# Layer 4 of a four-layer attention kernel: units of one batch and two heads, and values as three passes of high and low parts

## The chip, the core and the metric

The kernel runs on one core of a Trainium2 chip. Time is device time in microseconds for one execution of the whole program. A core has TensorE (matmuls and transposes into PSUM banks), VectorE, ScalarE and GpSimd, which work beside each other and are ordered by semaphores alone; SyncE issues the DMAs that stream weights in.

## What is computed

Four layers, each an attention block and a feed-forward block, over x of shape 8 x 128 x 512 and a context of the same shape. Only the fourth attention is touched:

```python
hidden_states = concatenate([context, latents], axis=1)       # 256 keys per batch
q = (latents @ Wq).reshape(b, q_len, N_KV_HEADS, N_GROUPS, HEAD_DIM)   # 4 x 8 heads of 128
k = (hidden_states @ Wk).reshape(b, kv_len, N_KV_HEADS, HEAD_DIM)
v = (hidden_states @ Wv).reshape(b, kv_len, N_KV_HEADS, HEAD_DIM)
scores = einsum('bqhgd,bkhd->bhgqk', q, k) / sqrt(HEAD_DIM)
out = einsum('bhgqk,bkhd->bqhgd', softmax(scores), v)
x = x + tanh(g_xattn[3]) * (out.reshape(b, q_len, 32 * 128) @ Wo)
```

Eight query heads in a row share one head of keys and values (a group); there are four groups. Behind it stands the last feed-forward block, a product with a dequantised 512 x 512 matrix.

## The kernel before

Products that need float32 precision are made in two ways. A full float32 matmul (`mm` with float32 operands) takes two records in the trace. `mm3` takes three matmuls of the reduced type `F32R`: each operand is split into a high part (a rounding copy) and a low part (the rest), and high by low, low by high and high by high are summed in PSUM. Layer 4 makes queries, scores and output with `mm3`, and values with full float32 matmuls of 128 moving columns.

Weights come as chunks of 128x512 through a ring of eight (`RING`): SyncE loads `raw`, GpSimd makes `w_hi` and `w_lo` (lines 614, 618), and TensorE frees a chunk by `w_free`, counted in `owed` and told on one of the next matmuls.

Layer 4 (`n == 3` in the code, `ATT[3]`, named L3) is cut into 128 units: a head by two batches, four units to a head. `run_steps` runs steps 0 to 129. In step k every engine goes through its own fixed list:

- TensorE (`attention(n)`, `step`): `scores(k)` into bank `S[k % 2]`; `turn(k - 1)`, four transposes of the probabilities into the bank `turned` (T); half a query piece (two of four contraction tiles, six matmuls of 512 columns) for a later head, in steps 0 to 123; `output(k - 2)`, two tiles of six matmuls together; `values(k - 1)` into the bank `value` (V).
- ScalarE: `pT` out of T for unit k-1 (line 1304), two exponentials for unit k (line 1519), in odd steps `q_hi`, then `a_hi` out of V for unit k-1.
- VectorE: `top`, the row maxima of unit k (line 2024); in four steps at each change of group a split of two batches of keys, `keys_split` (lines 1903, 1905); `reciprocal` and `g_inv` of unit k-1 (2046, 2049); two additions to `x` for unit k-2 (1970); `a_lo` for unit k-1 (2069); in odd steps `q_lo` (1911). At the end come the statistics of finished tiles (`tail_stats`, line 1703), the scale of the last norm for tiles 0 to 3 (`norm_scale`) and its first rows.

The waits that matter: values wait for `pT` and for the `a_hi` and `a_lo` of the unit before, since V is one bank; output waits for `a_hi` and `a_lo` of its own unit and for the addition that freed its bank; scores wait for `split`, which counts the split pieces of keys and queries in VectorE's order.

## Time and profile before

| | us |
|---|---|
| median of 3 runs | 2762.68 (2758.40 to 2764.48) |
| the profiled execution | 2762.54 |
| its span in the profile | 2760.7 |
| TensorE busy (matmuls) | 2682.1, 97% |
| VectorE busy | 1776.6, 64% |
| ScalarE busy | 1122.1, 41% |
| GpSimd busy | 839.7, 30% |

Layer 4's units run from 2105.5 to about 2722 us of the span; the last feed-forward block ends it. A busy share says that an instruction was in flight, not that the engine was at its peak. Durations of matmuls overlap: how far apart they start is the pace.

### The profile page before, as it was taken

What the parts mean: (1) busy time and instruction counts of PE and PEld (TensorE: products, weight loads), DVE (VectorE), ACT (ScalarE), POOL (GpSimd) and SP (SyncE); (2) the same over time, 40 slices, a digit from 0 to 9 for tenths busy, and PEclk for the clock granted to TensorE, in tenths of its full rate; (3) what the DMA queues carried; (4) which work ended last, traced back from release to release, by engine and by line L of the source; (5) the groups of instructions that cost most, each with busy time, mean ns of one, the idle gap of its engine ahead of it and who ended that gap; (6) DMA issues with size and microseconds to landing.
All of it is one profiled execution on the core that took longest, in us unless ns stands there. A gap on an engine that the chain in (4) does not pass through costs nothing.

```text
span 2760.7 us, 45251 instructions
## 1 busy us (share of the span) xinstructions
PE 2682.1 (97%) x14736; PEld 2264.1 (82%) x14736; DVE 1776.6 (64%) x3493; ACT 1122.1 (41%) x3088; POOL 839.7 (30%) x715
## 2 busy tenths in 40 slices
PE   6998999999999999999999999999999999999998
PEld 5886888888888887777888888788878888888887
DVE  5766545546446447777999999845553666666667
ACT  3542433333333333135666666421123444444442
POOL 4003433334324424323223222245523222222200
PEclk9999999999999999999999999999999999999999
DMA  5002111101101101111111111012211101110000
GB/s 149 17 5 67 43 35 50 38 29 51 42 23 53 42 27 46 37 38 39 31 34 30 34 30 33 29 47 61 58 45 40 28 28 28 32 28 28 28 5 31
DMA packets 59789, 106.01 MB, mean 38 GB/s; under 512 B 7184, under 2 KB 11536, under 8 KB 59536
## 3 DMA queue, kind: packets, MB, share of 16 engines
q1 hardware_dynamic: 56448, 96.49, 12.5%
q10 hardware_dynamic: 3216, 7.81, 0.8%
q8 instruction: 83, 1.36, 0.2%
q14 instruction: 42, 0.34, 0.0%
HBM read 100.09 MB, written 2.10 MB: 37 GB/s over the span
## 4 chain that ended last, share of the span: by engine, by line
PE 91%; DVE 6%; ACT 1%; issue 1%; POOL 1%; DMA 0%; DVEq 0%; ACTq 0%; POOLq 0%
PE four L651 50%; PE outp L651 25%; PE value L651 9%; PE turned L1016 4%; PE turned L773 1%; DVE stats L1703 1%; DVE x L1970 1%; PE value L698 0%; PE turned L698 0%; DVE probs L1732 0%; DVE nt L1665 0%; DMA raw<-in_stream 0%; PE turned L651 0%; DVE xt_lo L1737 0%; DVE probs L1850 0%
## 5 line engine op out<-in xcount | busy, mean ns | idle before, releaser
L614 POOL TENSOR_TENSOR w_hi<-raw,zero 128x512 fp32r<-128x512 f32 x347 | 372.6, 1074 | 1742.7 <-PE four L651 569.0
L1970 DVE SCALAR_TENSOR_TENSOR x<-outp,g_inv,x 128x512 f32<-128x512 f32 x768 | 548.6, 747 | 329.5 <-PE outp L651 328.6
L618 POOL TENSOR_TENSOR w_lo<-raw,w_hi 128x512 fp32r<-128x512 f32 x352 | 455.6, 1294 | 31.3 <-ACT w_hi L1304 4.2
L651 PE MATMUL four<-xt_hi,w_lo 128*128 128x512 f32 x1024 | 428.0, 418 | 3.9 <-DVE xt_lo L1737 3.2
L651 PE MATMUL four<-xt_hi,w_hi 128*128 128x512 f32 x1024 | 403.1, 394 | 0.0
L651 PE MATMUL four<-xt_lo,w_hi 128*128 128x512 f32 x1024 | 401.7, 392 | 0.0
L651 PE MATMUL outp<-w_hi,a_lo 128*128 128x512 f32 x800 | 327.1, 409 | 19.6 <-DVE a_lo L2069 10.4
L651 PE MATMUL outp<-w_hi,a_hi 128*128 128x512 f32 x800 | 316.7, 396 | 0.0
L651 PE MATMUL outp<-w_lo,a_hi 128*128 128x512 f32 x800 | 316.3, 395 | 0.0
L1519 ACT ACTIVATE probs<-probs,top 128x128 f32<-128x128 f32 x512 | 199.6, 391 | 213.6 <-DVE top L2014 127.4
L1304 ACT ACTIVATE pT<-turned 128x512 f32<-128x512 f32 x320 | 193.1, 603 | 203.4 <-PE turned L1016 145.6
L1304 ACT ACTIVATE a_hi<-value 128x512 fp32r<-128x512 f32 (+1 forms) x256 | 125.5, 490 | 339.1 <-PE value L651 339.1
L651 PEld LDWEIGHTS four<-xt_hi,w_hi 128*128 128x128 f32 x1024 | 192.9, 188 | 44.2
L2069 DVE TENSOR_TENSOR a_lo<-value,a_hi 128x512 fp32r<-128x512 f32 (+1 forms) x256 | 142.6, 557 | 129.0 <-ACT a_hi L1304 128.1
L651 PEld LDWEIGHTS four<-xt_hi,w_lo 128*128 128x128 f32 x1024 | 193.7, 189 | 36.8 <-issue 3.6
L651 PEld LDWEIGHTS four<-xt_lo,w_hi 128*128 128x128 f32 x1024 | 194.2, 190 | 31.1
L651 PEld LDWEIGHTS outp<-w_hi,a_lo 128*128 128x128 f32 x800 | 150.1, 188 | 83.5 <-issue 27.3
L651 PEld LDWEIGHTS value<-pT,v 128*128 128x128 f32 x1536 | 202.0, 192 | 17.2
L651 PE MATMUL value<-pT,v 128*128 128x128 f32 x1536 | 203.1, 275 | 0.0
L651 PEld LDWEIGHTS outp<-w_hi,a_hi 128*128 128x128 f32 x800 | 150.8, 189 | 36.8
L651 PEld LDWEIGHTS outp<-w_lo,a_hi 128*128 128x128 f32 x800 | 150.8, 189 | 29.0
L651 PE MATMUL four<-w_hi,ct_lo 128*128 128x512 f32 x416 | 167.2, 402 | 0.0
(299 smaller groups left out, 4911.1 us busy)
## 6 DMA issues: line engine op xcount, KB each, us to landing
raw<-in_stream SPq DMA_DIRECT2D x352, 256.0 KB, 2.6
ctx_raw<-in_ctx_t ACTq DMA_DIRECT2D x4, 512.0 KB, 6.2
x<-in_x_in ACTq DMA_DIRECT2D x2, 1024.0 KB, 10.6
kz<-kT SPq DMA_DIRECT2D x32, 64.0 KB, 2.7
pb<-in_position_bias ACTq DMA_DIRECT2D x1, 2048.0 KB, 9.2
out<-x SPq DMA_DIRECT2D x8, 256.0 KB, 2.0
qw<-in_qweight ACTq DMA_DIRECT2D x1, 768.0 KB, 3.9
ln_w<-in_ln_weight ACTq DMA_DIRECT2D x1, 256.0 KB, 2.6
```

The costliest lines, as they stand in the source:

```text
L614: pool.tensor_tensor(w_hi[:, k, :], raw[:, k % RAW, :], zero[:, :].to_broadcast([P, D]), ALU.add)\
L618: pool.tensor_tensor(w_lo[:, k, :], raw[:, k % RAW, :], f32(w_hi[:, k, :]), ALU.subtract)\
L651: m = pe.matmul(out_, l, r, start=start, stop=stop, skip_group_check=True)
L773: m = pe.transpose(T[:, tokens(j)], buf["pr"][:, u % 3, cols], ident[:, :])
L1016: m = pe.transpose(T[:, tokens(j)], probs[:, k % 2, tokens(j)], ident[:, :])
L1304: return act.activation(dst, src, ACT.Copy)
L1519: e = act.activation(probs[:, k % 2, cols], src[:, cols], ACT.Exp, bias=top[:, k % 2, j:j + 1], scale=1.0, accum_out=sums[:, k % 2, j:j + 1])
L1703: dve.bn_stats(stats[:, b, :], x[:, b, :]).then_inc(ln_tiny, 1)
L1970: dve.scalar_tensor_tensor(out=x[:, b, :], in0=O[no_f(k) % 2][:, :], scalar=scale, in1=x[:, b, :], op0=ALU.mult, op1=ALU.add)\
L2069: dve.tensor_tensor(buf["a_lo"][:, 0:w], V[:, 0:w], f32(buf["a_hi"][:, 0:w]), ALU.subtract).then_inc(s["a_lo"], 1)
```

## The change

1. A unit of layer 4 is now one batch and two heads that share keys and values: eight units to a pair of heads, still 128 units. Scores of a unit are two heads by the same 256 keys; output adds two tiles, from two weight chunks, to the same tile of `x`.
2. Query pieces are made in an order of pairs, in four slots; three instead of two are made ahead of step 0. The weight ring carries q, q, o, o for a pair instead of q, o for a head.
3. The values of a unit become one product of 256 moving columns (two heads by 128 queries) for each of two key tiles, as `mm3`: six matmuls of the reduced type instead of four full float32 products of 128 columns.
4. For that the turned probabilities get a high part (ScalarE's copy, now written as `F32R`) and a low part (`turned_lo`, a new subtraction on VectorE), and the values are split too (`values_split`, 16 pairs of a cast and a subtraction on VectorE). Values wait for `split` instead of `pT`. The split of keys stands behind the gate and `turned_lo` now.
5. `v_hi` lies over the space of `kT`, `v_lo` over that of `v`; the bias of the last block lies in the first keys and is loaded at step 34 instead of ahead of step 0.
6. The scale of the last norm for tiles 0 to 3 is made in step 127 instead of 128.

The diff, cut to its core:

```diff
@@ class Attention
-        self.NU = heads * units
+        self.together = 2 if name == "L3" else 1
+        self.NU = heads // self.together * units
-        self.nb = B // units
+        self.nb = self.together * B // units
@@
+            for i in range(self.NU + 1):
+                order += [("pT", i - 1)] if i else []
+                order += self.keys_split(i) + self.values_split(i) + self.pieces(i)
@@ prologue
-            self.first += vx[:4] + [w[0], w[1]] + vx[4:6] + [w[2], w[3]] + vx[6:] + q
+            self.first += vx[:4] + [w[0], w[1]] + vx[4:6] + [w[2], w[3]] + vx[6:]
+            self.first += [("q", 0, 0), ("q", 1, 0), ("q", 0, 1)]
@@ parts, splits
-        return [("q", t // 2, t % 2 * 2, 2)]
+        return [("q", self.query_piece(i)[1], i % 2 * 2, 2)]
+    def query_piece(self, i):
+        group, odd = divmod(i // 2 + self.ahead, 2)
+        return 2 * (group // 2) + odd, group % 2
+    def slot(self, what):
+        _, h, t = what
+        return (2 * (h // 2 * 2 + t) + h % 2) % 4
-        group, pair = divmod(i + 1, 8 * self.U)
-        return [("k", group, pair)] if i + 1 < self.NU and group and pair < 4 else []
+        group, at_ = divmod(i + 1, 4 * self.U)
+        return [("k", group, at_ // 2)] if i + 1 < self.NU and group and at_ in (0, 2, 4, 6) else []
+    def values_split(self, i):
+        group, at_ = divmod(i, 4 * self.U)
+        return [("v", group, at_ // 2)] if i < self.NU and at_ in (0, 2, 4, 6) else []
@@
-       Attention("L2", HEADS, 2, 8), Attention("L3", HEADS, 4, 0)]
+       Attention("L2", HEADS, 2, 8), Attention("L3", HEADS, 8, 0)]
@@ TensorE, scores
-                        for j, b in enumerate(L.batches(k)):
-                            cols = tokens(b % (B // 2))
+                        cols = tokens(b % (B // 2))
+                        for j, hd in enumerate(heads):
+                            slot = L.slot(("q", hd, b // 4))
@@ TensorE, turn
+                        if n == 3:
+                            pe.wait_ge(s["split"], L.split[("pT", k - 1)])
@@ TensorE, values
-                    elif k == 0:
-                        pe.wait_ge(s["j_out"], max(L.evac[("Vc", 0, B - 1)], L.evac[("Vx", 0, B - 1)]))
+                    else:
+                        group, b = k // (4 * L.U), k % L.U
+                        pe.wait_ge(s["split"], max(L.split[("pT", k)], L.split[("v", group, b // 2)]))
+                        for kt in range(2):
+                            both = slice(kt * 2 * P, (kt + 1) * 2 * P)
+                            m = mm3(V[:, 0:2 * P], (v_hi(group, b)[:, tokens(kt)], v_lo(kt, b, group)),
+                                    (buf["pT_hi"][:, both], buf["pT_lo"][:, both]), kt == 0, kt == 1, last=kt == 1)
+                        m.then_inc(s["values"], 1)
+                        return
...
-                            else:
-                                v = buf["v"][:, kt, b, tokens(h // 8)]
@@ ScalarE
-                        if kt == 0:
-
-                            act.wait_ge(FS[3]["wn"], 4)
-                            act.dma_start(M3["bias"][:, :], q_bias).then_inc(phase_in["F3"], 16)
-                        copy(buf["pT"][:, 0, :], T[:, :]).then_inc(s["pT"], 1)
+                        copy(buf["pT_hi"][:, :] if n == 3 else buf["pT"][:, 0, :], T[:, :]).then_inc(s["pT"], 1)
+                    if n == 3 and k == 4 * L.U + 2:
+                        act.dma_start(M3["bias"], q_bias).then_inc(phase_in["F3"], 16)
@@ VectorE
+                def values_split(what):
+                    _, group, pair = what
+                    rows = slice(2 * pair, 2 * pair + 2)
+                    v = buf["v"][:, :, rows, tokens(group)]
+                    hi = buf["v_hi"][:, group, rows, :].rearrange("p b (k t) -> p k b t", k=2)
+                    lo = buf["v_lo"][:, :, rows, tokens(group)]
...
+                    dve.tensor_copy(hi, v).then_inc(s["split"], 1)
+                    dve.wait_ge(s["split"], L.split[what] - 1)
+                    dve.tensor_tensor(lo, v, f32(hi), ALU.subtract).then_inc(s["split"], 1)
+                def turned_lo(u):
+                    dve.wait_ge(s["pT"], u + 1)
+                    dve.tensor_tensor(buf["pT_lo"][:, :], T[:, :], f32(buf["pT_hi"][:, :]), ALU.subtract)\
+                        .then_inc(s["split"], 1)
@@ VectorE, additions to x
+                        back = B if n < 3 else 1 if j else 2 * B - 1
-                        if no_f(k) > B:
-                            dve.wait_ge(s["x_acc"], at(L, lambda i: no_f(i) - B, k, it))
+                        if no_f(k) > back:
+                            dve.wait_ge(s["x_acc"], at(L, lambda i: no_f(i) - back, k, it))
@@ VectorE, tail_stats
+                        if n == 3 and k == L.NU - 1:
+                            norm_scale(range(B // 2), ln_base(norm + 1) + 6)
                         if n == 3 and k == L.NU:
-                            norm_scale(range(B // 2), ln_base(norm + 1) + 6)
@@ VectorE, step
-                    if n == 3 and k < L.NU:
+                    if 1 <= k <= L.NU:
+                        scaled_gate(k - 1, it, small)
+                    if n == 3:
+                        if 1 <= k <= L.NU:
+                            turned_lo(k - 1)
                         for what in L.keys_split(k):
                             keys_split(what)
-                    if 1 <= k <= L.NU:
-                        scaled_gate(k - 1, it, small)
+                        for what in L.values_split(k):
+                            values_split(what)
```

## Rows read from the trace of the kernel before

**Rows 1.** Page, chain that ended last, by engine: share of the span.
```profile
PE 91%; DVE 6%; ACT 1%; issue 1%; POOL 1%; DMA 0%; DVEq 0%; ACTq 0%; POOLq 0%
```

**Rows 2.** Busy time by stretch: length, each engine's busy us, granted clock, DMA share, GB/s.
```profile
2300.00:2500.00 200.00, 200.00 (x1245) 177.90 (x1245) 129.22 (x278) 91.11 (x269) 48.65 (x42) 1.00 0.10 27
```

**Rows 3.** Timeline of TensorE, one step: start, us, engine, line, operation, form.
```profile
2299.14 1.05 PE L651 MATMUL value<-pT,v 128*128 128x128 f32 x8
2299.95 0.36 PE L651 MATMUL four<-k_hi,q_lo 128*128 128x256 f32 x1
2300.15 0.28 PE L651 MATMUL four<-k_lo,q_hi 128*128 128x256 f32 x1
...
2300.74 0.60 PE L1016 MATMUL turned<-ident,probs 128*128 128x128 f32 x4
2301.10 0.48 PE L651 MATMUL four<-xt_hi,w_lo 128*128 128x512 f32 x1
...
2302.57 0.40 PE L651 MATMUL outp<-w_hi,a_lo 128*128 128x512 f32 x1
...
2303.98 1.05 PE L651 MATMUL value<-pT,v 128*128 128x128 f32 x8
```

**Rows 4.** Timeline of TensorE: last query piece ahead of step 0, then step 0.
```profile
2102.79 0.39 PE L651 MATMUL four<-xt_hi,w_lo 128*128 128x512 f32 x1
...
2105.51 0.28 PE L651 MATMUL four<-k_hi,q_lo 128*128 128x256 f32 x1
...
2106.23 0.39 PE L651 MATMUL four<-xt_hi,w_lo 128*128 128x512 f32 x1
```

**Rows 5.** Instructions by line and form, 2104 to 2760: busy us, mean ns, idle before.
```profile
L1737 DVE TENSOR_TENSOR xt_lo<-turned,xt_hi 128x512 fp32r<-128x512 f32 x4 | 2.7, 682 | 0.1
L1903 DVE CAST k_hi<-kT 128x512 fp32r<-128x512 f32 x12 | 5.0, 418 | 0.0
L1905 DVE TENSOR_TENSOR k_lo<-kT,k_hi 128x512 fp32r<-128x512 f32 x12 | 8.3, 693 | 0.4
L1703 DVE BATCH_NORM_STATS2 stats<-x 128x6 f32<-128x512 f32 x8 | 5.1, 680 | 0.0
```

**Rows 6.** Timeline of VectorE over the same step and into the next.
```profile
2300.65 0.42 DVE L2069 TENSOR_TENSOR a_lo<-value,a_hi 128x256 fp32r<-128x256 f32 x1 [0.55 <-ACT a_hi L1304]
2300.99 0.68 DVE L2024 TENSOR_REDUCE top<-four 128x2 f32<-128x512 f32 x1
2301.59 0.15 DVE L2046 RECIPROCAL inv<-sums 128x2 f32<-128x2 f32 x1
2301.78 0.23 DVE L2049 TENSOR_SCALAR g_inv<-inv,gate 128x2 f32<-128x2 f32 x1
2303.53 1.41 DVE L1970 SCALAR_TENSOR_TENSOR x<-outp,g_inv,x 128x512 f32<-128x512 f32 x2 [1.52 <-PE outp L651]
...
2305.83 0.68 DVE L1911 SCALAR_TENSOR_TENSOR q_lo<-four,q_hi 128x512 fp32r<-128x512 f32 x1
```

**Rows 7.** Timeline of ScalarE in the same step.
```profile
2300.23 0.39 ACT L1304 ACTIVATE a_hi<-value 128x256 fp32r<-128x256 f32 x1 [1.74 <-PE value L651]
2301.38 0.60 ACT L1304 ACTIVATE pT<-turned 128x512 f32<-128x512 f32 x1 [0.76 <-PE turned L1016]
```

**Rows 8.** Timelines of the layer's end: TensorE (step 122, last output), then VectorE.
```profile
2691.45 0.36 PE L651 MATMUL four<-k_hi,q_lo 128*128 128x256 f32 x1
...
2720.90 0.47 PE L651 MATMUL outp<-w_hi,a_lo 128*128 128x512 f32 x1 [1.13 <-DVE a_lo L2069]
...
2720.23 0.42 DVE L2069 TENSOR_TENSOR a_lo<-value,a_hi 128x256 fp32r<-128x256 f32 x1 [0.40 <-ACT a_hi L1304]
...
2724.08 1.00 DVE L1732 TENSOR_SCALAR probs<-x,mv,rstd 128x512 f32<-128x512 f32 x2
...
2727.51 0.67 DVE L1737 TENSOR_TENSOR xt_lo<-turned,xt_hi 128x512 fp32r<-128x512 f32 x1
```

**Rows 9.** Timeline of TensorE, first matmuls of the last block.
```profile
2730.70 0.63 PE L651 MATMUL outp<-wT_lo,xt_hi 128*128 128x512 f32 x1
```

More of the change, by code:

```diff
@@ L79, in early_chunks, with batches @@
         return []
+    def batches(self, i):
+        return list(range(B))
 class Attention:
@@ L111, in __init__ @@
                 u = i - self.lag_o
-                for b in self.batches(u):
-                    self.tile[(u, b)] = len(self.tile) + 1
+                for j in range(self.nb):
+                    self.tile[(u, j)] = len(self.tile) + 1
                 if u % self.U == self.U - 1:
-                    self.order.append(("o", u // self.U))
+                    self.order += [("o", h) for h in self.unit_heads(u)]
             if name == "L2":
@@ L123, in __init__ @@
         if name == "L3":
-            order = [("k", 0, pair) for pair in range(4)] + [("q", 0, 0), ("q", 0, 1)]
-            for i in range(self.NU):
-                order += self.keys_split(i) + self.pieces(i)
+            order = [("k", 0, pair) for pair in range(4)] + self.first[-self.ahead:]
+            for i in range(self.NU + 1):
+                order += [("pT", i - 1)] if i else []
+                order += self.keys_split(i) + self.values_split(i) + self.pieces(i)
             done = 0
             for what in order:
-                done += 2 if what[0] == "k" else 1
+                done += 2 if what[0] in "kv" else 1
                 self.split[what] = done
@@ L351, in build @@
             M3["u"] = sb("u", [P, KT, D], I32, st)
-        M3["bias"] = sb("q_bi", [P, D])
-        sb("behind_bias", [P, (KT - 1) * D])
+        q_lo = sb("q_lo", [P, 4, HALF], F32R)
         with ExitStack() as st:
@@ L381, in attention_buffers @@
         def attention_buffers(stack, n):
-            queries = {"qT": sb(f"qT{n}", [P, 2, TOK], F32, stack)} if n < 3 else \
-                {"q_hi": sb("q_hi", [P, 2, HALF], F32R, stack), "q_lo": sb("q_lo", [P, 2, HALF], F32R, stack)}
+            if n == 3:
+                return {
+                    "q_hi": sb("q_hi", [P, 4, HALF], F32R, stack),
+                    "q_lo": q_lo,
+                    "pT_hi": sb("pT_hi", [P, D], F32R, stack),
+                    "pT_lo": sb("pT_lo", [P, D], F32R, stack),
+                    "a_hi": sb("a_hi3", [P, 2 * P], F32R, stack),
+                    "a_lo": sb("a_lo3", [P, 2 * P], F32R, stack),
+                }
             return {
-                **queries,
+                "qT": sb(f"qT{n}", [P, 2, TOK], F32, stack),
                 "pT": sb(f"pT{n}", [P, 1, D], F32, stack),
@@ L437, in build @@
             A3 = attention_buffers(st, 3)
+            with ExitStack() as over:
+                A3["v_hi"] = sb("v_hi", [P, 4, B, 2 * P], F32R, over)
             A3["kT"] = sb("kT3", [P, 4, B, 2 * P], F32, st)
+            with ExitStack() as over:
+                A3["v_lo"] = sb("v_lo", [P, 2, B, D], F32R, over)
             A3["v"] = sb("v3", [P, 2, B, D], F32, st)
@@ L441, in build @@
             A3["k_lo"] = k_lo
+            M3["bias"] = A3["kT"][:, 0, 0:2, :].rearrange("p b t -> p (b t)")
             M3["sc"] = sb("q_sc", [P, KT], F32, st)
@@ L976, in scores @@
                     if n == 3:
-                        pe.wait_ge(s["split"], max(L.split[("q", h, t // 2)], L.split[("k", h // 8, t)]))
+                        heads, m, b = L.unit_heads(k), k // (4 * L.U), t
+                        pe.wait_ge(s["split"], max([L.split[("k", m, b // 2)]]
+                                                   + [L.split[("q", hd, b // 4)] for hd in heads]))
                     else:
@@ L1056, in output @@
                             continue
[L1057 removed]
+                        no = L.tile[(k, j)]
+                        if n == 3:
+                            c = chunk(lambda i: ("o", L.unit_heads(i)[j]), k, it)
                         if no > 2:
[L1060 removed]
+                            pe.wait_ge(s["x_acc"], at(L, lambda i: L.tile[(i, j)] - 2, k, it))
                         a = buf["a_hi"][:, tokens(j)], buf["a_lo"][:, tokens(j)]
                         mm3(O[no % 2][:, :], a, ring(c), True, True, last=True).then_inc(s["outp"], 1)
[L1063 removed]
+                        if n == 3 and k % L.U == L.U - 1:
+                            owed[0] += 1
+                    if n < 3 and k % L.U == L.U - 1 and len(L.batches(k)) - 1 in tiles:
                         owed[0] += 1
@@ L1433, in leave_bank @@
                     if kind == "q" and n == 3:
-                        dst, scale = buf["q_hi"][:, part, :], q_scale_
+                        dst, scale = buf["q_hi"][:, L.slot(what), :], q_scale_
                     elif kind == "q":
@@ L1699, in tile_stats @@
                     L = ATT[n // 2]
-                    dve.wait_ge(AS[n // 2]["x_acc"], max(t for (u, tb), t in L.tile.items() if tb == b))
+                    dve.wait_ge(AS[n // 2]["x_acc"], max(t for (u, j), t in L.tile.items() if L.batches(u)[j] == b))
                 else:
```

37 lines of the change are left out of this document (26 added, 11 removed).

## The prediction

> **What bounds the kernel now.** I read four views in this order. The chain of work that ended last says who decides the end: TensorE for 91% of the span, VectorE for 6% [rows 1]. The view by stretches, taken over 200 us of layer 4, shows TensorE busy for 200.00 of 200.00 us, VectorE for 129, ScalarE for 91, GpSimd for 49, at a granted clock of 1.00, which is the level of 2.4 GHz [rows 2]. So in this layer every other engine waits for TensorE, and what shortens TensorE's stream shortens the kernel until another chain becomes longer. The timeline of one step then gives the prices. A step is what TensorE issues for one unit: scores of unit k, transposes of unit k-1, half a query piece, output of unit k-2, values of unit k-1. I number steps from 0; there are 128 units.
>
> TensorE's step, by starts [rows 3]: values 2299.14 to 2299.95 (0.81 us, eight records for four products), scores 2299.95 to 2300.74 (0.79), transposes to 2301.10 (0.36), query half to 2302.57 (1.47), output to 2303.98 (1.41). From values to values that is 4.84 us; the same pattern repeats at 4.83 up to step 123. Durations in the rows are longer than these distances, since matmuls overlap; I use distances between starts for TensorE, and for VectorE wherever operations follow closely.
>
> **The values (the main term).** Removed: four products of 128 moving columns in full float32, 0.81 us. Added: two key tiles times three passes with 256 moving columns of the reduced type. Nothing like it writes the value bank now, but scores is the same form: 128 rows, 128 stationary columns, 256 moving columns, three passes of high and low parts, six in a row. There the first matmul takes 0.20 us to the second (2299.95 to 2300.15), the other five take 0.59 us up to the transposes, 0.118 each [rows 3]. The first one is the one that comes behind a full float32 matmul. In step 0 scores come behind a query matmul of the reduced type, and there all six take 0.72 (2105.51 to 2106.23), with no long first one [rows 4]. In the new order values come behind output and ahead of scores, all of the reduced type, so I take 0.118 for all twelve: 12 x 0.1175 = 1.41 us instead of 0.81 + 0.79 = 1.60. Gain 0.19 us a step. Bounds: 0.16 at step 0's pace, 0.10 if scores' first matmul keeps its 0.20, and 0.21 if the pace is a little better than the row.
>
> The trace has 0.118 us for a matmul of 256 columns of this kind at a clock of 1.00 [rows 3]. The Trainium skill (TensorE: Matmul & The Clock Gate, Back-to-back issue gap) gives 262 cycles at 2.4 GHz for 256 columns, 109 ns, and would make the six values 0.05 us shorter again, an estimate of some 6 us over the layer; the same rule misses scores as measured, so the row decides.
>
> The other parts of TensorE's stream keep their size. Scores now take two heads for one batch instead of one head for two batches: six loads and six matmuls as before. Output takes two tiles from two ring chunks instead of two tiles from one. The transposes write to other columns, 0.36 us either way. Query work is the same 64 pieces, but three instead of two are made before step 0: that is one piece more there, 2.72 us by the last piece ahead of step 0 (2102.79 to 2105.51 [rows 4]), and one fewer inside, so queries stop after step 121 instead of after step 123.
>
> **The low part of the turned probabilities (added work and a new wait).** VectorE gets one subtraction of 128x512 from the turned bank per step, and TensorE's values wait for it. The same operation on the same bank exists: xt_lo from turned, 682 ns [rows 5]; close behind others it costs 0.60, as top does (2300.99 to 2301.59); q_lo has top's duration and is taken alike [rows 6]. Queued behind it on VectorE: the splits, the two additions to x, a_lo, q_lo, top of the next unit. Who waits: values, and through x_acc and a_lo the next output.
> Is it in time? Let scores of step k start at 0; the new step is 0.705 scores, 0.36 transposes, 1.47 query, 1.41 output, 0.705 values, 4.65. Turned starts at 0.70; pT starts 0.64 behind it and takes 0.60 [rows 3, 7], so 1.94. VectorE comes from a_lo of unit k-2: values started at -0.70, their new length to the eviction is 0.91 (five distances of 0.118, 0.28 for the last, and the 0.04 that stands between the end of the values and a_hi now [rows 3, 7]), a_hi to a_lo 0.42 [rows 6, 7], so a_lo at 0.62, then 0.34, q_lo 0.60 in every second step, top 0.60, reciprocal and g_inv 0.33 [rows 6]: 2.5 at the latest. The subtraction ends at 3.15 and, with the 0.25 that TensorE takes from a_lo's end (2720.23 + 0.42) to output's start 2720.90 [rows 8], values could start at 3.4. TensorE arrives at 3.95. Slack 0.5 us in a step with q_lo, 1.1 in the other. As a loop over values: 0.91 + 0.42 + 0.34 + 0.60 + 0.60 + 0.33 + 0.68 + 0.25 = 4.13 against 4.65. So it costs nothing; without that cover each tenth beyond 0.5 costs 0.1 in every second step.
>
> The two additions now go to the same x tile, so the second waits for the first. They take 1.41 for both, and the first ends before the second output tile does (output tiles are 0.70 apart); a wait of VectorE on itself shows as 0.04 (reciprocal end 2301.75 to g_inv 2301.78 [rows 6]). I take 0.1 on VectorE, hidden. VectorE's step is then 0.34 + 0.60 + 0.33 + 0.60 + 1.5 + half of 0.60, 3.7 of 4.65.
>
> **The splits.** Values are split in 16 pairs of a cast and a subtraction. The keys' pair is the row: 418 and 693 ns [rows 5], at most 1.11. At each of three changes of group, key and value pairs alternate over eight steps, so VectorE has 3.7 + 1.1 = 4.8 in these steps against 4.65: up to 0.15 x 8 = 1.2 us of lag, spread over waits which have 0.3 to 0.8 us of room (the subtraction ends at 3.15 or 2.6, the first output tile at 3.4). Key pairs fall into steps where no q_lo stands ahead of top: 2.6 + 1.1 = 3.7, plus 0.25, ahead of the 4.65 at which scores need them. I take 0; the upper bound is 1.2 x 3 = 4 us.
>
> Other edits: the bias load moves to ScalarE's queue at step 34, into the dead part of the keys; it is one issue, and ScalarE is busy 91 of 200 us [rows 2]. The weight ring gets q, q, o, o instead of q, o; four chunks come free together at step 9 of each pair, while four others are ready, and GpSimd is busy a quarter of the time [rows 2]. Both nothing.
>
> **The start.** Step 1 needs the first subtraction: transposes at T, pT at T + 0.64, 0.60, subtraction 0.68, 0.25: 2.2 behind the transposes, TensorE arrives after 0.36 + 1.47 = 1.8 (no output yet). Loss 0.3.
>
> **The last steps.** Steps 122 to 127 have no query half: TensorE needs 3.2 and the loop decides. With one row of statistics (0.60 close behind others, 680 alone [rows 5]) in place of q_lo the loop is 4.13, as above. Measured from the start of step 122 (before: 2691.45 [rows 8]): values(121) 3.4; values(126) 3.4 + 5 x 4.13 = 24.0; in step 127 the norm's scale (2.2 us: from a_lo 2720.23 less 0.34 and two statistics of 0.60 to rows at 2724.08 is 2.3 [rows 8]) comes in, and top goes: values(127) at 24.0 + 4.13 + 2.2 - 0.6 = 29.8. Then a_lo 1.33 later, last output start 31.7 (before 29.45 = 2720.90 - 2691.45). From a_lo, before: 0.34, two statistics, scale, two rows of norm, two additions, two statistics, to xt_lo at 2727.51, 36.06 from step 122 [rows 8]. After: a_lo at 31.1, 0.34, one statistic, two rows of norm 0.95, and the additions, of which the second has to wait for the last output tile (31.7 + 1.65, so it runs from about 33.8 to 34.6), one statistic, xt_lo at 35.2. So the last stage starts 0.9 earlier than the old tail would give, though the last output is later: the scale has left the path. What is late next there is xt_lo itself and then row 2 of the norm, as now.
>
> **Sum.** Steps 2 to 121: 120 x 0.19 = 22.8. Step 1: +0.19 - 0.3 = -0.1. Query piece ahead: -2.7. Tail: +0.9. Together 20.9 us off the profiled execution's own 2762.54 (span 2760.7 and 1.8 around it), which stands at the median of the runs, 2762.68: 2741.7, I say 2742.
>
> **Rivals.**
> 1. The switch stays (chance 0.06). If the 0.20 of scores' first matmul comes from something other than its neighbour's type, 120 x 0.10 = 12.0 - 1.9 = 10 us: 2752. For: inside the steady steps the trace shows scores behind one kind of neighbour alone. Against: step 0 [rows 4].
> 2. VectorE cannot follow in places (0.12). The splits lag as bounded and the tail takes 0.5 us more in each of six steps: 4 + 3 = 7 us, 2749. For: VectorE has little idle time in those steps. Against: the reckoning of the waits above.
> 3. The slower one (0.04): the subtraction becomes the loop. Place: VectorE between pT and values. With q_lo the loop is 4.13 + d; from d = 0.52 it costs, and the average of a step passes the old 4.83 when 4.13 + d is 5.01, d = 0.88: the subtraction would have to take 1.56 instead of 0.68 us. At d = 1.3: 5.43 and 4.83 in turn, 5.13, 120 x 0.30 = 36 us slower, 2798. Against: 682 ns for the same form from the same bank [rows 5].
> 4. The gain is larger (0.10). 0.21 a step, and the last stage's first matmuls run at full pace: they take 0.63 us each now, where output's take about 0.40, ten such rows [rows 9], so 10 x 0.23 = 2.3. 25.2 - 2.8 + 0.9 + 2.3 = 25.6, 2737. For: the idle stretch ahead of them shrinks. Against: it does not go.
> 5. The edit does not reach the hardware as it reads, and nothing moves (0.02): 2760, within 0.2%.
>
> My forecast has 0.66. **Range:** 2736 to 2752 takes in rivals 1, 2 and 4 and leaves out 3 and 5 and what I have not seen. About 0.2% (5.5 us) is what a measurement of this kernel can tell from no change. Faster 0.94, same 0.02, slower 0.04.
>
> **What would show it.** In the timeline: values as six matmuls 0.118 apart, scores' six taking 0.705, a step of 4.65, no idle TensorE before values. Turned_lo at 0.68 us, ending half a microsecond before values start. In the waits: none of TensorE for VectorE in steps 2 to 121; in the last six, values waiting for pT_lo and steps of about 4.1. Wrong: a scores group that still takes 0.79, TensorE waiting for k_lo, or a step other than 4.6 to 4.7.

## The result, and the profile after

The changed kernel takes 2747.0 us (median of five runs, 2744.1 to 2748.9), the one before 2761.9 us on the same chip (2758.4 to 2764.5): ratio 0.9946, 95% interval 0.9935 to 0.9957. It ran twice more beside later experiments: 0.9954 (0.9941 to 0.9967) and 0.9950 (0.9937 to 0.9964). So it is faster by 0.5%, 11 to 15 us by the medians of the three comparisons; that is little, but every interval ends below 1. The forecast was 2742 with a range of 2736 to 2752. A single execution far off all others (8267.8 us, in the experiment with the low part for 8 of 512 columns) is in no figure here.

| | before | after |
|---|---|---|
| median, us | 2761.9 | 2747.0 |
| span of the profiled execution, us | 2760.7 | 2747.1 |
| start of step 0 of layer 4 | 2105.51 | 2109.98 |
| step 0, step 1 | 2.09, 3.83 | 2.09, 5.08 |
| steps 2 to 121, 120 steps | 580.02 | 564.37 |
| start of step 122 to the end | 69.25 | 65.58 |

The first three lines behind the span are read from the timeline of TensorE, as starts of the scores of a step; the last is the rest of the span. Between the two profiles lie -13.6 us: +4.5 up to step 0, +1.2 in steps 0 and 1, -15.7 in steps 2 to 121, -3.7 from step 122 on. Two later profiles of the same changed kernel differ from this one in three of these lines (below): step 1, steps 2 to 121 and the end.

The chain that ended last, by engine, of the changed kernel (it answers to [rows 1]), shows a little less TensorE and a little more VectorE:

```profile
PE 89%; DVE 7%; ACT 1%; issue 1%; POOL 0%; ACTq 0%; DMA 0%; DVEq 0%; POOLq 0%
```

Busy time by stretch, in the columns of [rows 2]: TensorE is still busy all the time at a granted clock of 1.00; VectorE has risen from 129 to 171 us in 200.

```profile
2300.00:2500.00 200.00, 199.88 (x1198) 174.75 (x1197) 171.07 (x335) 93.19 (x275) 53.65 (x45) 1.00 0.10 30
```

One step of TensorE after the change (it answers to [rows 3]):

```profile
2300.61 0.28 PE L698 MATMUL value<-pT_hi,v_lo 128*128 128x256 f32 x1
2300.72 0.28 PE L698 MATMUL value<-pT_lo,v_hi 128*128 128x256 f32 x1
...
2301.32 0.28 PE L698 MATMUL four<-k_hi,q_lo 128*128 128x256 f32 x1
2301.43 0.28 PE L698 MATMUL four<-k_lo,q_hi 128*128 128x256 f32 x1
...
2302.02 0.60 PE L1069 MATMUL turned<-ident,probs 128*128 128x128 f32 x4
2302.38 0.48 PE L698 MATMUL four<-xt_hi,w_lo 128*128 128x512 f32 x1
...
2303.85 0.39 PE L698 MATMUL outp<-w_hi,a_lo 128*128 128x512 f32 x1
...
2305.26 0.28 PE L698 MATMUL value<-pT_hi,v_lo 128*128 128x256 f32 x1
```

Six values take 0.71 us (2300.61 to 2301.32), six scores 0.70, and the long first matmul of scores, 0.20 in [rows 3], is gone. From values to values it is 4.65; over a long run of undisturbed steps 4.655. Nothing stands in brackets: TensorE waits for nothing.

The same step on VectorE (it answers to [rows 6]), with the new subtraction in it:

```profile
2300.16 1.61 DVE L2054 SCALAR_TENSOR_TENSOR x<-outp,g_inv,x 128x512 f32<-128x512 f32 x2 [0.33 <-issue]
2301.93 0.42 DVE L2158 TENSOR_TENSOR a_lo<-value,a_hi 128x256 fp32r<-128x256 f32 x1 [0.16 <-ACT a_hi L1367]
2302.28 0.68 DVE L2109 TENSOR_REDUCE top<-four 128x2 f32<-128x512 f32 x1
...
2303.29 0.69 DVE L1995 TENSOR_TENSOR pT_lo<-turned,pT_hi 128x512 fp32r<-128x512 f32 x1
2304.82 1.60 DVE L2054 SCALAR_TENSOR_TENSOR x<-outp,g_inv,x 128x512 f32<-128x512 f32 x2 [0.83 <-PE outp L698]
```

The subtraction ends at 2303.98, 1.28 us ahead of the values at 2305.26; in a step with q_lo it would be some 0.6 later, and still in time.

What was not foreseen is seen in the groups of VectorE from 2110 to 2680 us, by form; the last number before the bar is the mean in ns:

```profile
L1995 DVE TENSOR_TENSOR pT_lo<-turned,pT_hi 128x512 fp32r<-128x512 f32 x121 | 83.0, 686 | 0.1
L2138 DVE TENSOR_SCALAR g_inv<-inv,gate 128x2 f32<-128x2 f32 x121 | 36.2, 299 | 4.3
L1990 DVE TENSOR_TENSOR v_lo<-v,v_hi 128x512 fp32r<-128x512 f32 x16 | 14.3, 896 | 0.5
L1967 DVE TENSOR_TENSOR k_lo<-kT,k_hi 128x512 fp32r<-128x512 f32 x12 | 10.5, 872 | 0.4
```

k_lo was 693 ns before the change [rows 5]; its mean is now 872, and v_lo, of the same form, has 896. pT_lo, which reads PSUM beside its SBUF operand, is at 686 as forecast. Three of the twelve k_lo and three of the sixteen v_lo are long where the group changes, and one more v_lo at the start of the layer. VectorE and GpSimd in steps 33 and 34, first VectorE:

```profile
2264.38 0.42 DVE L1965 CAST k_hi<-kT 128x512 fp32r<-128x512 f32 x1
2264.82 1.41 DVE L1967 TENSOR_TENSOR k_lo<-kT,k_hi 128x512 fp32r<-128x512 f32 x1
...
2270.28 1.24 DVE L1988 CAST v_hi<-v 128x512 fp32r<-128x512 f32 x1
2271.56 1.65 DVE L1990 TENSOR_TENSOR v_lo<-v,v_hi 128x512 fp32r<-128x512 f32 x1
```

and GpSimd, which splits the weight chunks:

```profile
2264.52 1.16 POOL L661 TENSOR_TENSOR w_hi<-raw,zero 128x512 fp32r<-128x512 f32 x1 [6.33 <-PE outp L698]
2265.76 1.61 POOL L665 TENSOR_TENSOR w_lo<-raw,w_hi 128x512 fp32r<-128x512 f32 x1
...
2270.20 1.04 POOL L661 TENSOR_TENSOR w_hi<-raw,zero 128x512 fp32r<-128x512 f32 x1 [0.45 <-DMA raw<-in_stream]
2271.32 1.35 POOL L665 TENSOR_TENSOR w_lo<-raw,w_hi 128x512 fp32r<-128x512 f32 x1
```

Read them in turn. w_hi (1.04 alone, 1.16 here) ends at 2265.68; k_lo is recorded from 2264.82 to 2266.23, which is about the wait for that end and then its own 0.69. w_lo (1.29 alone) is recorded from 2265.76, waits for k_lo to end and takes 1.61. The cast v_hi waits for w_hi, and v_lo for w_lo. In each of these four the record is 0.14 to 0.15 us shorter than the wait plus the instruction's own time, so the sum holds to that much. One whole instruction waits for the other, and the record of the waiting one begins while it waits. The steps that hold this are 4.78 (33), 5.00 (34), 6.41 (35), 4.85 (36) and 4.82 us (38) long; in step 35 the output waited 1.17 us for a_lo:

```profile
2275.16 0.48 PE L698 MATMUL outp<-w_hi,a_lo 128*128 128x512 f32 x1 [1.17 <-DVE a_lo L2158]
```

The same is found at steps 65 to 70 and 97 to 102, though step 67 is 5.34 where step 35 is 6.41. In all, steps 2 to 121 take 564.37 where 120 x 4.655 is 558.6: 5.8 us lost. The Trainium skill (SBUF — State Buffer, SBUF: two separate sides) has a rule for it: VectorE and GpSimd share a pair of SBUF ports under an exclusive lock, which whichever instruction starts first holds to its end; on VectorE's side it concerns an instruction in a mode with two ports, or one with two SBUF inputs beside a GpSimd instruction that reads SBUF. By that rule k_lo and v_lo, with two SBUF inputs, are subject to it, and pT_lo, which has one input in PSUM, is free of it; the trace agrees (1.41 to 1.65 us for the subtractions that waited, 0.69 alone, and 0.68 to 0.69 for every pT_lo, GpSimd at work or not). The casts were stretched too, up to 1.24; by the rule they would be in a mode with two ports, which no row shows directly.

### The profile page after: what moved, and what is told of

Its sections match the earlier page's. It is cut to its first block, busy times and chain, and to the rows that moved or that the text cites. A ratio compares the mean times of both kernels' runs of the same rounds, so it can differ in the third digit from the quotient of the medians.

```text
span 2747.1 us, 45163 instructions
## 1 busy us (share of the span) xinstructions
PE 2664.0 (97%) x14480; PEld 2238.0 (81%) x14480; DVE 1893.6 (69%) x3653; ACT 1123.7 (41%) x3088; POOL 844.6 (31%) x715
## 4 chain that ended last, share of the span: by engine, by line
PE 89%; DVE 7%; ACT 1%; issue 1%; POOL 0%; ACTq 0%; DMA 0%; DVEq 0%; POOLq 0%
PE four L698 50%; PE outp L698 24%; PE value L698 9%; PE turned L1069 4%; PE turned L820 1%; DVE x L2054 1%; DVE stats L1765 1%; PE value L745 0%; PE turned L745 0%; DVE probs L1794 0%; DVE nt L1727 0%; ACT a_hi L1367 0%; DVE a_lo L2158 0%; PE turned L698 0%; DVE pT_lo L1995 0%
## 5 line engine op out<-in xcount | busy, mean ns | idle before, releaser
L2054 DVE SCALAR_TENSOR_TENSOR x<-outp,g_inv,x 128x512 f32<-128x512 f32 x768 | 560.0, 748 | 251.1 <-PE outp L698 225.9
L698 PEld LDWEIGHTS outp<-w_hi,a_hi 128*128 128x128 f32 x800 | 150.3, 188 | 35.9
L698 PE MATMUL four<-w_hi,ct_hi 128*128 128x512 f32 x416 | 163.1, 392 | 0.0
L698 PE MATMUL four<-w_lo,ct_hi 128*128 128x512 f32 x416 | 162.8, 391 | 0.0
L1367 ACT ACTIVATE pT<-turned 128x512 f32<-128x512 f32 x192 | 115.9, 604 | 106.9 <-PE turned L820 57.9
```

The lines of the kernel that those rows point to most:

```text
L698: m = pe.matmul(out_, l, r, start=start, stop=stop, skip_group_check=True)
L1367: return act.activation(dst, src, ACT.Copy)
L2054: dve.scalar_tensor_tensor(out=x[:, b, :], in0=O[no_f(k) % 2][:, :], scalar=scale, in1=x[:, b, :], op0=ALU.mult, op1=ALU.add)\
```

## The experiments

Ten more runs followed the first comparison, two of them of the changed kernel itself. The theory (A) was: the loop is TensorE's at 4.655, and what the sum lacks is lost where VectorE's splits meet GpSimd's. Its rivals: (B) VectorE has too little room for eight pairs of splits in some eight steps, whoever else works; (C) the gain comes from the units and the columns rather than from the passes; (D) the subtraction is not hidden at all.

### GpSimd kept away from the splits

```diff
+            def holds(k):
+                return 31 <= k < 103 and (k + 1) % 32 < 8
...
-                            owed[0] += 1
+                            (held if holds(k + L.lag_o) else owed)[0] += 1
```

A chunk that comes free in steps 31 to 38, 63 to 70 or 95 to 102 is handed on only after them.

> The changed kernel, but TensorE holds back the release of weight chunks that fall into steps 31 to 38, 63 to 70 and 95 to 102 until the step behind them, so GpSimd has no chunk to split while VectorE splits keys and values; VectorE's work is the same, eight splits in a row. Theory A (a split with both operands in SBUF, or the cast ahead of it, waits for GpSimd): k_lo and v_lo stay at 0.69 us instead of up to 1.65, the steps 33 to 38 take 4.65 to 4.75 instead of 4.78 to 6.41, and layer 4 gets about 5 us shorter: 2742. Rival B (VectorE simply falls behind with 1.1 us more in eight steps in a row): these steps stay between 4.8 and 5.3, at most 1.1 us is won: 2746.

Measured: 2746.6 us, ratio 0.9949 (0.9932 to 0.9966), so the median came out at B's 2746 and not at A's 2742. The trace says otherwise: steps 31 to 39 are all 4.65 to 4.66, steps 2 to 121 take 559.8 instead of 564.4. The groups of VectorE from 2255 to 2289.5 us:

```profile
L1975 DVE TENSOR_TENSOR k_lo<-kT,k_hi 128x512 fp32r<-128x512 f32 x4 | 2.8, 693 | 0.1
L1998 DVE TENSOR_TENSOR v_lo<-v,v_hi 128x512 fp32r<-128x512 f32 x4 | 2.8, 693 | 0.1
```

GpSimd has nothing to do from 2234.9 to 2289.8 there. Eight pairs in eight steps cost nothing with GpSimd idle, so B falls and A stands. A new loss of 0.35 us came at step 40 (also 72 and 104), where GpSimd makes up for its rest. There a VectorE operation on two columns, 0.23 us long elsewhere, waited behind GpSimd and made pT_lo late:

```profile
2296.40 1.14 DVE L2146 TENSOR_SCALAR g_inv<-inv,gate 128x2 f32<-128x2 f32 x1
2297.45 0.68 DVE L2003 TENSOR_TENSOR pT_lo<-turned,pT_hi 128x512 fp32r<-128x512 f32 x1
```

```profile
2296.22 1.30 POOL L665 TENSOR_TENSOR w_lo<-raw,w_hi 128x512 fp32r<-128x512 f32 x1
```

The median, on another chip than the first comparison's, shows 0.4 us of the 4.6 us that the steps win in the trace. Its four runs lie between 2743.7 and 2749.0, and its profiled execution took 67.9 us from step 122 to the end where the changed kernel's took 65.6, since its clock fell there (more of that below). So the steps carry the verdict here, not the median; that the time follows is shown only by the last experiments.

### The new units with values in full float32

```diff
-                            m = mm3(V[:, 0:2 * P], (v_hi(group, b)[:, tokens(kt)], v_lo(kt, b, group)),
-                                    (buf["pT_hi"][:, both], buf["pT_lo"][:, both]), kt == 0, kt == 1, last=kt == 1)
+                            m = mm(V[:, 0:2 * P], buf["v"][:, kt, b, tokens(group)], buf["pT_hi"][:, both],
+                                   kt == 0, kt == 1)
```

with turned_lo and values_split left away; the units, the query order and the ring of the change stay.

> The new units, query order and ring, but values as two full float32 matmuls of 256 moving columns, with no low part and no split of values. Theory: the gain is in the passes, not in the units or the 256 columns. Values take 0.81 to 0.86 us, scores' first matmul takes 0.20 again, a step is 4.83 to 4.88; against the kernel before the start loses 2.7 and the tail gives back 1 to 4 us: 2760 to 2768. Rival: 256 moving columns alone make it shorter, values 0.7 us or less, step 4.7, some 2748.

Measured: 2757.1 us, ratio 0.9981 (0.9971 to 0.9991), 3 us below the forecast; the step is 4.81, also a little below it. TensorE's values and the first two scores:

```profile
2303.85 1.03 PE L697 MATMUL value<-pT_hi,v 128*128 128x256 f32 x4
2304.53 0.47 PE L697 MATMUL four<-k_hi,q_lo 128*128 128x256 f32 x1
2304.83 0.28 PE L697 MATMUL four<-k_lo,q_hi 128*128 128x256 f32 x1
```

Values take 0.68 and scores' first matmul 0.30: 1.58 for both against 1.60 before. So 0.02 of the step is due to units and columns and 0.155 to the passes: six passes take 0.03 more than these values, and the long first matmul of scores, 0.18 over the pace here, goes. The rival was right that values take less than 0.7 us, but the first matmul of scores took 0.10 back, so C falls for the steady step. What pays there is that no full float32 stands between matmuls of the reduced type any more.

For the whole time C keeps a share. This kernel is 4.3 us below the one before, about a third of what the change gains: 2.8 us in steps 2 to 121 (577.2) and 5.5 from step 122 on (63.7), where a step takes 3.48 against 3.66 before and 4.10 in the changed kernel, less what is lost ahead of step 0. So the low part costs the changed kernel some 4 us from step 122 on (67.9 in its profiles with the clock fallen at the end, as it fell here), and what the units and the moved scale of the norm give there is several times the forecast's net +0.9. Why the new units shorten a step there from 3.66 to 3.48 was not looked into.

### The low part for 8 of 512 columns

```diff
-                    dve.tensor_tensor(buf["pT_lo"][:, :], T[:, :], f32(buf["pT_hi"][:, :]), ALU.subtract)\
+                    w = slice(0, 8 if u else D)
+                    dve.tensor_tensor(buf["pT_lo"][:, w], T[:, w], f32(buf["pT_hi"][:, w]), ALU.subtract)\
```

> The changed kernel, but from unit 1 on the low part of the turned probabilities is made for 8 of 512 columns, so the rest of it is stale; 0.5 us less on VectorE per step. Theory: VectorE is no bound in the steady steps, which stay at 4.655; the last six steps fall from 4.10 to 3.55, step 1 is unchanged (unit 0 is made whole), the changes of group lose less: 2747 - 3 - 3 = 2741. Rival: VectorE or the wait of values holds the steady steps, which then fall to 4.6 or less: 2735.

Measured: 2735.2, 2737.6 and 2741.7 us (forecast 2741), ratio 0.9924 (0.9903 to 0.9945). The steady step stays 4.655: the full subtraction is hidden there, and D falls. Where VectorE is the loop it shows: steps 122 to 126 take 3.57 instead of 4.10, so 0.53 is what all but 8 columns of the subtraction cost uncovered. The changes of group lost nothing either (4.65 to 4.66 in steps 32 to 39), although GpSimd splits as in the changed kernel: all k_lo and v_lo take 0.69. VectorE's work comes at other moments now and meets GpSimd elsewhere; VectorE, then GpSimd:

```profile
2264.29 0.86 DVE L2139 TENSOR_SCALAR g_inv<-inv,gate 128x2 f32<-128x2 f32 x1
...
2265.59 0.69 DVE L1990 TENSOR_TENSOR v_lo<-v,v_hi 128x512 fp32r<-128x512 f32 x1
```

```profile
2263.83 1.29 POOL L665 TENSOR_TENSOR w_lo<-raw,w_hi 128x512 fp32r<-128x512 f32 x1
2265.59 1.59 POOL L661 TENSOR_TENSOR w_hi<-raw,zero 128x512 fp32r<-128x512 f32 x1 [0.46 <-DMA raw<-in_stream]
```

Here v_lo was first and kept its 0.69, and w_hi waited: 1.59 instead of 1.04.

### The subtraction twice

```diff
+                    dve.tensor_tensor(buf["pT_lo"][:, :], T[:, :], f32(buf["pT_hi"][:, :]), ALU.subtract)\
+                        .then_inc(s["split"], 1)
+                    dve.wait_ge(s["split"], L.split[("pT", u)] - 1)
                     dve.tensor_tensor(buf["pT_lo"][:, :], T[:, :], f32(buf["pT_hi"][:, :]), ALU.subtract)\
```

> The changed kernel with the subtraction made twice, one behind the other: about 0.72 us more on VectorE between pT and values. By the prediction's slack of 0.5 us, steps with q_lo take 4.85 and the others 4.65, average 4.75, 60 x 0.2 = 12 us; the last six steps 4.8 each, 4 us; the changes of group, where VectorE then has 5.6 us of work per step, up to 20 us: 2747 + 36 = 2783. If the slack is really larger, 4.655 in the steady steps and 2771; if smaller, both kinds of steps get longer.

Measured: 2791.1 us, ratio 1.0115 (1.0094 to 1.0137), 8 us above the forecast. Steps with and without q_lo take 4.82 and 4.65 in turn, with ten of 5.4 and three of 5.17 outside the changes of group. Values wait for the second subtraction:

```profile
2303.46 0.36 PE L698 MATMUL value<-pT_hi,v_lo 128*128 128x256 f32 x1 [0.28 <-DVE pT_lo L1998]
```

This puts a number on rival 3 of the prediction. The second subtraction adds 0.72 (from start to start); 4.13 + 0.72 is 4.85, measured 4.82 (so the slack of 0.5 was rightly reckoned), and the last steps went from 4.10 to 4.82. So the loop over VectorE is 4.10 in the changed kernel, and a step with q_lo has 0.55 us of cover. Steps 2 to 121 take 600.3, 35.9 more, of which 60 x 0.17 = 10 us are the steps with q_lo; some 20 are at the changes of group, as forecast, where steps 31 to 39 are 5.2 to 6.3 us long; the steps of 5.4 were not foreseen.

### The changed kernel again, and the first values ahead of step 0

> The changed kernel once more, beside the three below, so that they are compared on the same chip. Nothing is altered. Expected: ratio to the kernel before 0.9946 again, within 0.001; step 1 about 5.1 us, steady steps 4.655, steps 33 to 38, 65 to 70 and 97 to 102 together 5.6 us over the even pace. The last block: its matmuls of 512 columns at 0.40 or at 0.63 us, by the granted clock of that execution; if the clock differs from that of the first profile, the 2.7 us that the end gained over the forecast are the execution's and not the change's.

Measured: 2749.1 us, ratio 0.9954 (0.9941 to 0.9967). With nothing altered, step 1 is 4.09 us and not 5.08. The changes of group lose 6.9 us and not 5.8, since step 67 is 6.44 here and was 5.34; the other long steps are the same to 0.02. In the first profile of the changed kernel, VectorE and GpSimd, and what TensorE made of it:

```profile
2112.89 1.56 DVE L1990 TENSOR_TENSOR v_lo<-v,v_hi 128x512 fp32r<-128x512 f32 x1
```

```profile
2112.86 1.04 POOL L661 TENSOR_TENSOR w_hi<-raw,zero 128x512 fp32r<-128x512 f32 x1 [0.29 <-DMA raw<-in_stream]
```

```profile
2116.36 0.36 PE L698 MATMUL value<-pT_hi,v_lo 128*128 128x256 f32 x1 [1.11 <-DVE pT_lo L1995]
```

In the second:

```profile
2113.16 0.69 DVE L1990 TENSOR_TENSOR v_lo<-v,v_hi 128x512 fp32r<-128x512 f32 x1
```

```profile
2113.29 1.46 POOL L661 TENSOR_TENSOR w_hi<-raw,zero 128x512 fp32r<-128x512 f32 x1 [0.45 <-DMA raw<-in_stream]
```

The chunk landed a little later, v_lo was first by 0.13 us, and the wait changed sides: GpSimd's cost nobody anything. Both of GpSimd's bracketed waits are for the chunk's DMA. So 1 us of step 1 hangs on the moment at which a transfer lands. My reading of 5.08 as a property of the kernel was wrong.

```diff
-            order = [("k", 0, pair) for pair in range(4)] + self.first[-self.ahead:]
+            order = [("k", 0, pair) for pair in range(4)] + [("v", 0, 0)] + self.first[-self.ahead:]
...
-        return [("v", group, at_ // 2)] if i < self.NU and at_ in (0, 2, 4, 6) else []
+        return [("v", group, at_ // 2)] if 0 < i < self.NU and at_ in (0, 2, 4, 6) else []
```

> The split of the first pair of values (a cast and a subtraction on VectorE, 0.42 and 0.69 us where nothing hinders them) is taken out of step 0, where GpSimd splits weight chunks, and put ahead of it, before the low part of the first query piece. Theory A (the two engines shut each other out): step 0 loses the cast of 0.84 and the subtraction of 1.56, the maximum of step 1 comes earlier by about their excess, and step 1 goes from 5.08 to 3.9 to 4.1 us; step 0 may start up to 1.1 us later, if the two operations are not covered by the query piece. Sum -1.0 (0 to -1.2) on a time of 2747. Theory B (step 1 is long because of the order of VectorE's work in it, whatever GpSimd does): step 1 keeps at least 4.6 us. The group changes are untouched and lose 5.6 us as before.

Measured: 2747.0 us, ratio 0.9948 (0.9935 to 0.9961); step 1 is 4.09 us. By itself that tells nothing, since the changed kernel reaches 4.09 as well. The moved pair still met GpSimd (the cast took 1.04 and the subtraction 1.66 us), but ahead of step 0, where the query pieces cover it. One profile can't show that step 1 is never 5.1 to 5.2 any more.

### Both remedies together, and VectorE's side moved instead

First the edit of the chunks and that of the first values in one kernel:

> Both remedies for the same cause: the first pair of values split ahead of step 0, and the chunks that are freed in steps 31 to 38, 63 to 70 and 95 to 102 handed to GpSimd only after the splits of keys and values in them. Expected if both losses come from GpSimd's splits beside VectorE's: step 1 4.0 us, steps 31 to 39 all 4.65, 0.35 us lost at each of steps 40, 72 and 104 (seen with the second remedy alone), so steps 0 to 122 take 1.0 + 4.6 = 5.6 us less than in the changed kernel, and the median is 2741 to 2742, ratio to the kernel before 0.9925. If the median shows less than 3 us against the changed kernel on the same chip, what the steps win is given back elsewhere (the end, or the granted clock), and the trace must show where.

Measured: 2745.7 us, ratio 0.9941 (0.9928 to 0.9954), 4 us above the forecast time, and 3.4 us below the changed kernel on the same chip; by the steps 5.4 (steps 2 to 121 take 560.1 against 565.5). It loses 0.5, 0.3 and 0.45 us at steps 40, 72 and 104 and 0.15 at 74. The 1 us of step 1 could not be won, since that profile of the changed kernel had 4.09 there already.

Then the chunks are left as the change has them, and the splits move (the first values stay ahead of step 0):

```diff
-        group, at_ = divmod(i + 1, 4 * self.U)
-        return [("k", group, at_ // 2)] if i + 1 < self.NU and group and at_ in (0, 2, 4, 6) else []
+        group, at_ = divmod(i + 4, 4 * self.U)
+        pair = {0: 0, 2: 1, 4: 2, 9: 3}.get(at_)
+        return [("k", group, pair)] if i + 4 < self.NU and group and pair is not None else []
```

and likewise `values_split`, with `i + 3` and `{0: 0, 2: 1, 7: 2, 9: 3}`.

> The other side of the same collision is moved: not GpSimd's splits of weights (the chunks are freed as in the changed kernel) but VectorE's splits of keys and values, out of steps 33 to 35 of each group's change: four of the eight to steps 28 to 31, the other ones to 32 and to 36 to 38; and the first pair of values is split ahead of step 0. Theory A (a lock between the two engines while both work from SBUF): the subtractions take 0.69 us at all or nearly all places, the changes of group lose at most 0.35 us in a few steps where a small operation of VectorE (g_inv, two columns) meets GpSimd's, and the median is 2741 to 2743. Rival (VectorE cannot take eight splits more in some ten steps, whatever GpSimd does): the steps that hold a split stay at 4.8 to 5.0 and 2 us or more are lost at each change.

Measured: 2742.5 us, ratio 0.9938 (0.9924 to 0.9952). Steps 33 to 39 are even; only steps 32, 64 and 96 are long, 5.13, which is 0.48 over the pace where at most 0.35 was expected. There the pair of step 31 still met a chunk; VectorE, then GpSimd:

```profile
2251.12 1.41 DVE L1994 TENSOR_TENSOR v_lo<-v,v_hi 128x512 fp32r<-128x512 f32 x1
```

```profile
2250.74 1.25 POOL L665 TENSOR_TENSOR w_hi<-raw,zero 128x512 fp32r<-128x512 f32 x1 [20.30 <-PE outp L702]
```

The last version puts the pairs into steps in which that trace shows GpSimd idle (`i + 5` with `{0: 0, 2: 1, 5: 2, 10: 3}` for keys, `i + 4` with `{0: 0, 2: 1, 8: 2, 10: 3}` for values):

> As the run before it (splits of keys and values out of steps 33 to 35, first pair of values ahead of step 0), but with the second pair of values out of step 31 too, where its subtraction took 1.41 us behind GpSimd's split of a chunk and step 32 became 5.13 us. Pairs now in steps 27, 28, 29, 30, 32 and 36 to 38 of each change of group; by the trace of the run before GpSimd is idle from 2230.4 to 2250.7 (steps 27 to 30) and from 2253.7 to 2260.4 (step 32). Theory (a whole-instruction lock between VectorE's splits and GpSimd's): all v_lo and k_lo of the changes 0.69 us, step 32, 64 and 96 at 4.65, steps 2 to 121 within 0.5 us of 120 times 4.655, 558.6, median 1 to 1.5 us lower than that kernel's, 2741. If the subtraction is long in other steps instead, the theory or my reading of where GpSimd works is wrong.

> The changed kernel a third time, as the comparison on the same chip. Nothing is altered: ratio to the kernel before 0.9950 within 0.001; steps 33 to 38 and the like lose 5.6 us again. Step 1 either 4.1 or 5.1 us, by whether GpSimd's next chunk has landed before VectorE's subtraction starts; the stretch from step 122 to the end either 65.6 us (granted clock 1.00 in it) or about 67.9 us (clock fallen).

Measured: 2741.8 us, ratio 0.9933 (0.9920 to 0.9946), against 2747.1 us, ratio 0.9950 (0.9937 to 0.9964), for the changed kernel on the same chip. Steps 2 to 121 take 558.9 against 565.5, and not one of them is off the pace. Its groups of VectorE from 2110 to 2680 us:

```profile
L1994 DVE TENSOR_TENSOR v_lo<-v,v_hi 128x512 fp32r<-128x512 f32 x15 | 10.4, 693 | 0.5
L1971 DVE TENSOR_TENSOR k_lo<-kT,k_hi 128x512 fp32r<-128x512 f32 x12 | 8.3, 693 | 0.4
```

It does the same work as the changed kernel, with the same matmuls, and only the steps of the splits differ. So the splits' loss is GpSimd's doing and is won back whole in the steps. In time, this version's interval lies wholly below 1, so it beats the kernel before; against the changed kernel it is 5.3 us better in the median, but the intervals of the two ratios overlap, and there the trace carries the verdict. Against the version ahead of it, which ran on another chip, its ratio is 0.0005 lower, which the intervals can't tell from none. In the third profile of the changed kernel the splits lost 6.9 us again, step 1 was 5.20 us, and from step 122 to the end it took 67.9.

## Why the prediction was right, and which terms were off

**The values.** Right. Six matmuls 0.118 apart, scores' first one at the same pace, nothing idle. The gain is 4.833 - 4.655 = 0.178 a step and not 0.19: I had taken single distances of one step (4.84) where the mean of 120 is 4.833. 120 x 0.178 is 21.4 for 22.8.

**Rival 1 (the switch stays)** did not happen: the first matmul of scores is 0.118 ahead of the second in the steady steps. The 262 cycles for 256 columns of the Trainium skill (TensorE: Matmul & The Clock Gate, Back-to-back issue gap), which the page gives for a single matmul without its weight load and which would have made the values 0.05 us shorter, are not seen either: the row decided rightly.

**The low part.** Right: 686 ns, no wait of TensorE for it in the undisturbed steps. The loop reckoned from rows was 4.13; the last steps, where nothing covers it, measure 4.10, and the kernel without most of the subtraction 3.57. The two additions to the same tile take 1.60 and not 1.5, hidden.

**The splits.** This is the term that failed. I took 0 with 4 as the upper bound, and it is 5.8 us in the first profile and 6.9 in the two others. The bound came from VectorE's capacity alone (4.8 us of work in a step of 4.65); the run with GpSimd held back shows that this part costs nothing. I took the pair's 1.11 us from rows in which GpSimd happened not to interfere [rows 5] and dismissed the ring's new order in a clause ("four chunks come free together ... nothing"). Both statements held by themselves. Together they put four chunks' worth of GpSimd splits on top of VectorE's, and the trace after shows 0.7 to 1 us more for each subtraction that meets one. The prediction's own signs show it: it said that TensorE waits nowhere for VectorE in steps 2 to 121, and named a step other than 4.6 to 4.7 as a sign of being wrong; the output of step 35 waits 1.17 us for a_lo, and fifteen steps are 4.77 to 6.41 long. "GpSimd is busy a quarter of the time" is a mean; the question was when.

**The start.** The query piece ahead is 2.72, as said. Step 1 was to be 0.1 longer. It is 0.26 longer in the one profile of the changed kernel in which v_lo came first, and 1.25 and 1.37 longer in the two in which it did not.

**The last steps.** 4.10 for 4.13; xt_lo comes 35.10 behind the start of step 122 for the 35.2 forecast (before 36.06 [rows 8]). The way there is right. Of the 3.7 us of the end, that is 0.96; most of the rest is not the change's. Rival 4 had the last stage's first matmuls at full pace, and in the first profile they are:

```profile
2719.65 0.40 PE L698 MATMUL outp<-wT_hi,xt_lo 128*128 128x512 f32 x1
```

where [rows 9] has 0.63. But in the second profile of the same kernel they are 0.63 as before, and so is the output ahead of them:

```profile
2713.55 0.63 PE L698 MATMUL outp<-w_hi,a_lo 128*128 128x512 f32 x1 [0.98 <-ACT a_hi L1367]
...
2721.30 0.63 PE L698 MATMUL outp<-wT_hi,xt_lo 128*128 128x512 f32 x1
```

The stretch there, in the columns of [rows 2], has a granted clock of 0.79 in the second profile (that is, the engine at 1.2 GHz for part of it and at 2.4 for the rest), with TensorE busy for 8.6 of 14 us. In the first profile, on the second line, the clock held at 1.00, with TensorE busy for 7.99 us:

```profile
2709.00:2723.00 14.00, 8.62 (x33) 6.61 (x32) 12.48 (x28) 2.07 (x4) 0.00 (x0) 0.79 0.00 1
2709.00:2723.00 14.00, 7.99 (x44) 6.59 (x45) 12.94 (x30) 2.67 (x5) 0.00 (x0) 1.00 0.00 1
```

The clock fell there in two of three profiles of the changed kernel (67.9 us from step 122 to the end; 65.6 where it held). With the clock fallen in both kernels, the end gains 69.25 - 67.9 = 1.35 us, near the 0.9 forecast, but not where the forecast had it: there xt_lo comes 35.85 to 35.89 behind step 122, only 0.2 before the 36.06 of the kernel before, whose clock fell behind its last output. So that the two numbers are near is in part luck. Rival 4 is a matter of the execution; the kernel before was profiled once, so whether its clock ever holds there is not known.

**The sum.** Forecast span 2760.7 - 20.9 = 2739.8, measured 2747.1: 7.3 us over. The splits 5.8, the pace 1.4, step 1 1.15, the layers ahead 1.75 (their code is the same; executions differ by this much there, step 0 of this kernel started between 2107.1 and 2110.3), less 2.8 at the end. The time fell into the range, on the side of rival 2, and that needed luck. Rival 2's total of 7 us matches the 7.3 only by chance: its 4 us for the splits were too little and came from the wrong reason, and its 3 us for the last steps did not come (4.10 against 4.13). And the top of the range, 2752, was set by rival 1, which did not happen either.

## What to carry to other kernels

Where a change gives VectorE work that reads SBUF alone, look not at GpSimd's share of busy time but at which of its instructions stand at the same moments; of two operations of 0.7 and 1.3 us that met, the second to start took its own time and what was left of the other's. Moving VectorE's splits by a few steps cost nothing here, while holding GpSimd's back cost 0.3 to 0.5 us at each place where it caught up. Bound such a term from the row in which both engines work, not from the clean row. And before a difference of 1 to 3 us at one place is explained, profile the same kernel twice: here step 1 and the end both changed by that much with nothing altered.

## What the runs showed of the hardware that was not expected

- A VectorE operation on two columns (g_inv, 0.23 us) took 0.86 and 1.14 us where it met a GpSimd instruction, and up to 1.23 in the changed kernel: the wait is for the other's end, as long for a short operation as for a long one.
- Which engine pays is decided by who starts first: w_hi was 0.03 us ahead of v_lo in the first profile and v_lo 0.13 ahead of w_hi in the second. The VectorE operations that read PSUM (pT_lo, top, q_lo) kept 0.68 to 0.69 us beside GpSimd's splits.
- A full float32 matmul of 256 columns pays no more per column than one of 128: values took 0.68 us as four records of 256 columns against 0.81 as eight of 128, but the first matmul of the reduced type behind it grew from 0.20 to 0.30, and the two together were 1.58 against 1.60.
